# Combine stage of a two-layer pair-mixing kernel: the sum over k for all 256 rows at once, both halves of the product kept on chip

## What is computed

```python
zn = layer_norm(z)                                  # over c
a  = m * sigmoid(zn @ w_ag + b_ag) * (zn @ w_ap + b_ap)
b  = m * sigmoid(zn @ w_bg + b_bg) * (zn @ w_bp + b_bp)
p  = einsum('bikc,bjkc->bijc', a, b)                # for each c: a 256x256x256 product
x  = layer_norm(p) @ w_z + b_z
g  = sigmoid(zn @ w_g + b_g)
out = z + x * g                                     # residual added in this stage
```

## Time and profile before

| | |
|---|---|
| median of 3 executions (lowest, highest) | 2308.48 us (2306.16, 2319.19) |
| the profiled execution: its time, its span | 2298.41 us, 2296.6 us |
| combine of layer 0: first piece of b asked for, last `add` ends | 312.16, 646.19 us |
| the same for layer 1 | 1376.60, 1704.92 us |
| fill, 16 steps of layer 0 | 315.5 to 363.8 us |
| mixed, 48 steps of layer 0 | to about 582 us |
| drain, 16 steps of layer 0 | to 646.2 us |
| mean length of L919 (128x512 written with 64 floats between neighbours) | 1.066 us |
| mean length of L924 (128x512 written side by side) | 0.613 us |
| mean length of L242, whose neighbours in a pair lie 64 floats apart | 0.281 us |
| mean length of L493 (`conv_project`), whose neighbours in a pair lie 256 floats apart | 0.282 us |
| `fold_weights` of layer 0: its one DMA issued, first use, first matmul, last operation begins | 2.37, 4.91, 5.31, 6.79 us |

### The profile page before, as it was taken

The page is one execution under the profiler, slowest core; times in us unless marked ns, Lnnn a source line. Parts: engine busy times, 40 slices in busy tenths (PEclk is TensorE's granted clock), DMA queues, the critical chain, the costliest instruction groups (busy, mean ns, idle before and its releaser), DMA issues. The chain is left out here.

```text
span 2296.6 us, 44402 instructions
## 1 busy us (share of the span) xinstructions
PE 1752.8 (76%) x11740; PEld 1164.1 (51%) x11740; DVE 1584.8 (69%) x5005; ACT 1142.8 (50%) x2610; POOL 1168.2 (51%) x1594
## 2 busy tenths in 40 slices
PE   5778748888646659838887737978746999999998
PEld 3444437778522238724444426877734444444443
DVE  6888704566757768838787730665664889889887
ACT  5898813333125549817676633333216545555541
POOL 5777604676857740026566520766765343444330
PEclk9999979999779989959999979999885999999999
DMA  3777547888633314958789746988764555555552
GB/s 115 204 193 190 156 137 240 273 297 284 209 117 93 95 51 82 191 179 242 233 252 267 217 115 179 311 276 272 260 193 144 155 157 158 155 158 160 153 140 68
DMA packets 475473, 423.19 MB, mean 184 GB/s; under 512 B 224690, under 2 KB 372402, under 8 KB 475314
## 3 DMA queue, kind: packets, MB, share of 16 engines
q1 hardware_dynamic: 402610, 303.87, 47.4%
q10 hardware_dynamic: 72704, 117.47, 15.2%
HBM read 236.68 MB, written 150.99 MB: 169 GB/s over the span
## 5 line engine op out<-in xcount | busy, mean ns | idle before, releaser
L699 PE MATMUL cp_pv<-cp_weight,cp_zt 64*128 64x320 f32 x2048 | 369.8, 469 | 103.4 <-ACT cp_zt L637 87.8
L257 POOL TENSOR_TENSOR cc_ln_rstd<-cc_ln_var,numbers 128x8 f32<-128x8 f32 x128 | 255.5, 1996 | 188.5 <-DVE cc_ln_var L248 179.6
L523 DVE SCALAR_TENSOR_TENSOR a_res<-cp_pv,cp_mask,cp_sig 128x64 f32<-128x64 f32 x1024 | 263.9, 322 | 123.9 <-ACT cp_sig L646 119.4
L1537 DVE TENSOR_TENSOR ex_xe<-ex_spread,ex_xd 128x512 f32<-128x512 f32 x512 | 322.6, 683 | 36.0 <-PE ex_spread L1779 35.8
L829 PE MATMUL cc_sum<-a_res,cc_bch 128*128 (+1 forms) x2048 | 297.9, 296 | 62.6 <-DMA cc_bch<-b_scratch 59.3
L919 ACT ACTIVATE cc_p<-cc_sum 128x512 f32 (+1 forms) x128 | 135.8, 1061 | 376.4 <-PE cc_sum L829 239.7
L829 PEld LDWEIGHTS cc_sum<-a_res,cc_bch 128*128 128x128 f32 x2048 | 269.8, 205 | 85.0 <-issue 76.1
L646 ACT ACTIVATE cp_sig<-cp_pv 128x384 f32<-128x384 f32 x512 | 249.7, 493 | 125.7 <-PE cp_pv L699 124.0
L699 PEld LDWEIGHTS cp_pv<-cp_weight,cp_zt 64*128 64x128 f32 x2048 | 184.3, 189 | 222.3 <-issue 193.7
L1796 PE MATMUL ex_po<-ex_xe,ex_expert 128*64 128x512 f32 x1024 | 267.8, 647 | 0.1
L1589 POOL TENSOR_TENSOR ex_rstd<-ex_var,numbers 128x8 f32<-128x8 f32 x64 | 104.7, 1636 | 270.4 <-DVE ex_var L1485 260.5
(11 more groups left out here) (186 smaller groups left out, 2976.4 us busy)
## 6 DMA issues: line engine op xcount, KB each, us to landing
cc_bch<-b_scratch SPq DMA_DIRECT2D x256, 256.0 KB, 3.9
gate_scratch<-cp_sig SPq DMA_DIRECT2D x128, 256.0 KB, 2.6
b_scratch<-cp_b_stage SPq DMA_DIRECT2D x128, 256.0 KB, 4.0
cc_g<-gate_scratch ACTq DMA_DIRECT2D x128, 256.0 KB, 4.5
after_conv<-cc_p ACTq DMA_DIRECT2D x128, 256.0 KB, 3.8
ex_xd<-ex_xt SPq DMA_DIRECT2D x256, 128.0 KB, 2.5
cp_x<-in_x SPq DMA_DIRECT2D x64, 256.0 KB, 3.3
cc_p<-in_x ACTq DMA_DIRECT2D x64, 256.0 KB, 3.6
```

Of the source, the lines that this page charges most:

```text
L257: pool.tensor_tensor(rstd[q][:], var[q][:], numbers[:, 0:1].to_broadcast([P, tiles]), ALU.pow).then_inc(scaled if shifts else known, 1)
L523: dve.scalar_tensor_tensor(a_res[:, h, :, row], bank[:, h, 3 * C:4 * C], mask_sb[:, h, row:row + 1], sig[u.mod(2)][:, 0, h, i, :], ALU.mul ...
L699: pe.matmul(pv[slot(u, i)][:, h, 0:COLS], zt[u.mod(2)][half, i * P:(i + 1) * P], weight[half, :], start=True, stop=True).then_inc(v_made, 1)
L1537: dve.tensor_tensor(xe[u.mod(2)][:, :, h, i * P:(i + 1) * P], pb[2 * (p % 2) + h][:].rearrange("p (e t) -> p e t", e=EP), xd[u.mod(8)][:, ...
```

## The change

p is now cut into the two halves of j alone. For each half a piece of b (two channels, `CHUNKS` = 32 pieces) meets all 256 rows i: four matmuls with 256 columns, so each piece of b is read once instead of twice. The first half's p goes into `ptile` (now 256 rows), the second half's over half 0 of `a_res`, channel by channel as the products are done with it (`take_sums`), so with 256 floats between the channels of a row. There are three phases: 32 pieces alone; 32 steps with a piece of the second half beside the norm of eight rows of the first; 32 steps with the norm of the second half. Six buffers `room` of 128 x 512 serve b in the first phase; in the second two of them serve b, one `pn`, one `pt` and two g; in the third `pn` and `pt` have two each.

Per four steps (`QUAD`, 32 columns) DVE makes a first guess of 1/sqrt by integer operations (`first_guess`), and POOL refines it by three Newton rounds (`newton`, twelve small operations), in place of four powers. `measure` runs six steps ahead (`LEAD`). The fetch of x moves from ACT's queue to SP's. `prepare_weights` becomes `fold_projection`: one DMA of a packed array, one block. The loops are written out.

```diff
+def newton(pool, numbers, guess, half_var, root, rstd, done, base):
+    three_halves = numbers[:, 2:3].to_broadcast(list(rstd.shape))
+    for k in range(3):
+        was = guess if k == 0 else rstd
+        for j, (out, a, b, op) in enumerate([(root, was, was, ALU.mult), (root, root, half_var, ALU.mult),
+                                             (root, root, three_halves, ALU.subtract), (rstd, was, root, ALU.mult)]):
+            if j or k:
+                pool.wait_ge(done, base + 4 * k + j)
+            pool.tensor_tensor(out, a, b, op).then_inc(done, 1)
...
+        def p_rows(n, i, count):
+            at = n % STEPS * SR + i
+            if n < STEPS:
+                return ptile[:, at:at + count, :]
+            return a_res[:, 0, :, at:at + count].rearrange("p c i -> p i c")
...
+                for k in range(CHUNKS + 2):
+                    load_b(k)
+                for n in range(STEPS):
+                    load_x(n)
+                    if n + 2 < CHUNKS:
+                        load_b(CHUNKS + n + 2)
...
-                        for c in range(CH):
-                            at = (j * CH + c) * TI
-                            for k in range(H):
-                                ins = pe.matmul(psum[q][:, at:at + TI], bch[buf][:, k, :, c],
-                                                a_res[:, k, bass.ds(s * SC + j * CH + c, 1), ih * TI:(ih + 1) * TI],
-                                                start=k == 0, stop=k == H - 1)
...
+                    for c in range(CH):
+                        for half in range(H):
+                            ins = pe.matmul(psum[k % 3][:, c * N:(c + 1) * N], b[:, half, :, c],
+                                            a_res[:, half, k % CHUNKS * CH + c, :], start=half == 0, stop=half == H - 1)
...
+                for k in range(CHUNKS):
+                    add_up(k)
+                for n in range(STEPS):
+                    add_up(CHUNKS + n)
+                    if n:
+                        project(n - 1)
+                    flip(n)
+                project(STEPS - 1)
+                for n in range(STEPS, LAST):
+                    flip(n)
+                    if n > STEPS:
+                        project(n - 1)
+                project(LAST - 1)
...
+                for half in range(H):
+                    for n in range(half * STEPS, half * STEPS + LEAD):
+                        measure(n)
+                    for n in range(half * STEPS, (half + 1) * STEPS):
+                        scale(n)
+                        if n + LEAD < (half + 1) * STEPS:
+                            measure(n + LEAD)
+                        if n % STEPS:
+                            gate(n - 1)
+                    gate(n)
...
+                for half in range(H):
+                    refine(half * STEPS // 4)
+                    for n in range(half * STEPS, (half + 1) * STEPS):
+                        if n % 4 == 2 and n + 4 < (half + 1) * STEPS:
+                            refine(n // 4 + 1)
+                        if n % STEPS:
+                            add(n - 1)
+                    add(n)
...
+                for n in range(STEPS):
+                    take_sums(CHUNKS + n)
+                    take_flipped(n)
+                    if n:
+                        store(n - 1)
```

More of the change, by code:

```diff
@@ L135, in _ @@
                     ins.then_inc(centered, 1)
[L138 to L217, removed]
@@ L763, in chunk @@
-        def chunk(at, j):
-            turn, number = at
-            return (number + j) % BUFS, turn * (TURN * SUBS // BUFS) + (number + j) // BUFS
-        def now(part, r, t, q):
-            if r > 0:
-                half = t + (r - 1) * (STEPS // 2)
-                part(half * 2 + q, half, q, r - 1)
-        def behind(part, r, t, q, first):
-            if r > 0 and not (r == 1 and first):
-                half = t + (r - 1) * (STEPS // 2) - (1 - q)
-                part(half * 2 + 1 - q, half, 1 - q, r - 2 if first else r - 1)
@@ L780, in before @@
[L780 to L794 removed]
+        counted, guessed, refined = m.sem("counted"), m.sem("guessed"), m.sem("refined")
@@ L880, in body, with measure @@
-                def body(r, t, q, first, last, at):
-                    before(measure, r, t, q, last)
-                    now(scale, r, t, q)
-                    behind(gate, r, t, q, first)
-                rounds(dve, body)
-                at_end(gate)
+                def measure(n):
+                    dve.wait_ge(p_made, CHUNKS if n < STEPS else 2 * CHUNKS)
+                    if n % 4 == 0 and n:
+                        dve.wait_ge(guessed, n // 4 * 3 - 2)
+                    for i in range(0, SR, 2):
+                        ins = dve.bn_stats(stats[:, n % 4, i:i + 2, :].rearrange("p t s -> p (t s)"),
+                                           p_rows(n, i, 2).rearrange("p t c -> p c t"))
+                    ins.then_inc(counted, 1)
+                    if n % 4 == 3:
+                        first_guess(n // 4)
@@ L893, in add, with refine @@
[L893 to L904 removed]
+                def refine(quad):
+                    pool.wait_ge(guessed, quad * 3 + 3)
+                    if quad >= 2:
+                        pool.wait_ge(pn_made, (quad - 1) * 4)
+                    newton(pool, numbers, guess[:].bitcast(F32), half_var[:], root[:],
+                           rstd[quad % 2][:].rearrange("p n i -> p (n i)"), refined, quad * ROOTS)
@@ L936, in body @@
-                def body(r, t, q, first, last, at):
-                    if first:
-                        behind(store, r, t, q, first)
-                        if 2 <= r < len(TILES):
-                            act.wait_ge(stored, 16 * STEPS * (r - 1))
-                    if r < len(TILES):
-                        take_sums(r, t * 2 + q, q)
-                    now(take_flipped, r, t, q)
-                    if not first:
-                        behind(store, r, t, q, first)
-                rounds(act, body)
```

322 lines of the change are left out of this document (191 added, 131 removed).

## The result

The changed kernel took 2327.49 us (median, 2323.69 to 2337.52), the kernel before beside it 2307.32 (2304.51 to 2319.19): ratio 1.0084, 95% interval 1.0043 to 1.0126, slower by some 19 us. The prediction said 2318, range 2265 to 2350, slower the likeliest of the three.

The account below looks back on a forecast made before the run. The landing of g, in its buffer's two-step round, was taken to bound mixed steps. Layers of 342.1 us add 8.1 and 13.8, less 2 x 6.0: +9.9, 2308.3; with 10.1 from profiled execution to median, 2318, range 2265 to 2350.

Parts of the forecast that it names:

- First phase and the way to the second: Start of combine: 32 pieces alone at 1.73 us, 60.8 us, then 9.8 us from last product to first flip.
- Preparation: Weights made ready before combine: 8.0 us in place of 14.0, 6.0 less a layer.
- Second phase: 32 steps of products beside norm: POOL's Newton operations delay one `add` in four by 1.8 us; 3.8 a step, 119.8 us.
- Rival 4: Products beside norm: PE sets the step, 3.45 us for 3.8, 22 us less in all, 2296 us; chance 0.12.
- From the second to the third phase: Between norms of the two halves: 3.3 us to `gate`, then 8.5 for measure, guess, Newton and `scale`; 11.8 us.
- the tail: End of combine after the last norm steps: 5.0 us a layer.
- `scale` of the second half: DVE reading neighbours 256 floats apart: no extra cost taken; the other end was 0.46 us more a step.
- Rival 3: Norm of the second half: strided read costs `scale` 0.46 us in each of 64 steps, 29 us, 2347 us; chance 0.08.
- Third phase: 32 steps of norm alone on the second half: 4.35 us a step on average, 134.9 us a layer.
- two thirds of it at 4.69: Norm of the second half: two thirds at half clock, 4.69 us a step, one third at full clock, 3.66.
- Rival 2: Norm of the second half: half clock throughout, 4.69 us a step for 4.35, 10.5 a layer more, 2339 us; chance 0.20.
- Rival 1: Norm of the second half: PE stays at full clock, 3.66 us a step for 4.35, 21.4 a layer less, 2275 us; chance 0.22.

Follow-up runs that it names:

- the last versions: Changed kernel with all gainful edits and `scale` walking p four floats at a time, 0.9651; more g buffers, 0.9561; extra products too, 0.9575; all against the kernel before.
- the run with the clock held: Changed kernel with five extra 128-column PE products a step while the second half is normed; ratio 1.001 to the kernel before.
- the fastest version: Changed kernel with all gainful edits, four-float `scale` reads, and four g buffers from step 8 beside the second half's products; 2202.35 against 2302.33 us for the kernel before, 0.9561.

## Why the prediction was nearly right, and where it was not

The direction was right with the sum 7 to 9 us short in each layer; the table names the terms.

- **First phase and the way to the second:** 70.8 and 70.4 for 70.6. Pieces of 1.73 at a clock of 1.00 after the start, and 9.6 us from the last product of the first half to the first flip (forecast 9.8).
- **Preparation:** 6.0 a layer, shown by the run with nothing else changed.
- **Second phase:** 121.2 and 119.8 for 119.8, by the mechanism named. The block made the `add` 1.9 late, and both runs without the block took 4 to 9 us a layer off (the 4 alone would not be clear of the spread named above). Rival 4 (PE-bound, 3.45 a step) fell with it: a step took 3.9, 3.6 to 3.7 without the block, and 3.45 only with more buffers of g as well.
- **From the second to the third phase:** 15.4 and 17.3 for 11.8. The failed step is "Last flip, copy, projection, `gate`: 1.34 + 1.40 + 0.6 = 3.3". It let gate(31) wait for its projection only. It waited 5.11 us for g, with the measuring behind it on DVE. With the measuring ahead the term is 11.1 and 12.1. The same omission is in the tail (7.7 and 6.4 for 5.0), where the last `gate` waits 1.77 for g in layer 0 and 0.49 in layer 1; that was not tested by itself, and four buffers took 1 to 2 us off it.
- **`scale` of the second half:** the failed step is "I take nothing". It is 1.00 for 0.68, which is 9.9 us in 31 steps, and with neighbours read 11 us a layer went. Rival 3, given a chance of 0.08, had the right premise, at 0.32 instead of 0.46. The row it leaned on, L493, was a poor witness: it takes 0.28 us for 128 elements whatever it reads, 2.2 ns each, and so may hide a read that holds `scale` to 1.00 us for 512, 1.96 ns each; that it does is argued, no run tests it. The Trainium skill ("Advanced Engine Details and Errata", SBUF Cachelines) asks for two hits on a line of 16 bytes; the runs agree: single floats 1 KB apart 1.00 us, two floats of each 16 bytes 0.68 (`scale` in the last versions, four floats to a jump of 1 KB), whole neighbours 0.68. They don't tell floats to a line from floats to a jump.
- **Third phase:** 136.2 and 135.3 for 134.9 is luck, two errors that offset each other. The steps were priced right but for the stride (4.63 and 3.15 with neighbours read, forecast 4.69 and 3.18), and so was the block: the run with the clock held has three steps of 3.47 and a long one of some 5.5, 15.9 in four (over all its steps 16.2), and the forecast's 14.6 with 4 x 0.32 is 15.9. The failed step beside the stride is "two thirds of it at 4.69". By the granted clock some 17 and 16 steps of 31 ran at half clock and not 21, and that took off about as much as the stride put on. Rival 2, half clock throughout, fell with it: the clock came back several times in each layer, though PE waits in every step, and mostly fell again in a long step of 5.5 to 5.8. That is the course that the prediction described, and not that of the rule on oscillation as it put it for this rival.
- **Rival 1 priced full clock at 21.4 a layer.** Held at 0.97 the phase gave 10: 3.66 a step left out the stride (3.66 + 0.32 = 3.98, measured 4.05), while the phase that it starts from was short by the share of half clock.
- **What the prediction did not see:** it named POOL's block in two phases and took it as the price of the change. Newton's twelve operations are shorter than four powers, 3.9 against 6.6 us, and yet the powers win by 30 us a layer: 6 in the ways between the phases, where the first `scale` waits for one power instead of the whole block, and 24 in the second and third phases, 49 in both layers. Newton cut in three parts wins 42 there, though it is as many operations. It is the block that costs, not the operations.

## What to carry to other kernels

Price work by where it stands in its engine's queue, not by its length: the twelve operations in one block cost some 50 us in the two phases, and 12 more on the ways between them, that a longer but evenly spread power did not. At a change of phase, write down each operation that stands behind a wait it doesn't need; DVE stood still for 5 us ahead of a measuring that had all it needed. And before a row stands in for the cost of an access, ask whether its operation is fast enough to be held up by it.

## What was unexpected of the hardware

- What a strided DVE read costs depends on how much it takes at each place: two floats of each 16 bytes, four to a jump, are enough for 0.68 us, and one float to a jump costs 1.00.
- Turning p for this has a price on PE, which is in the measured time of the fastest version: there a weight load of the flip takes 0.21 us at full clock where it takes every fourth float, and 0.14 where it takes neighbours (its own second phase).
- The strided read is paid twice: the `add` on POOL that starts 0.16 us behind `scale` takes 1.65 behind a `scale` of 0.68 and 1.93 behind one of 1.00, alone 1.26. Min, median and max of the two phases of the changed kernel:

```profile
L854 POOL TENSOR_TENSOR cc_p<-cc_p,cc_room x30: 1267/1644/1711, 384.6 to 497.0; 128x512 f32<-128x512 f32 x30
L854 POOL TENSOR_TENSOR cc_p<-cc_p,cc_room x30: 1262/1923/1942, 519.7 to 649.3; 128x512 f32<-128x512 f32 x30
```

- The power of 8 columns took 1.64 us where the kernel before has a mean of 2.00 (groups by line and shape). It isn't whether DVE is quiet: in the kernel before, the 178 powers that begin while a `scale`, or the like operation of the next stage, runs on DVE take 2.01 to 2.13, and the 14 others 1.63 to 1.65. With one power a step all 128 took 1.63 to 1.65, with `gate`, measuring and even a whole `scale` beside them, but none began inside a `scale`.

```profile
L257 POOL TENSOR_TENSOR cc_ln_rstd<-cc_ln_var,numbers 128x8 f32<-128x8 f32 x128 | 255.5, 1996 | 188.5 <-DVE cc_ln_var L248 179.6
```

- A clock at 0.97 instead of 0.70 gave 10 us in 136; at 0.92 instead of 0.83, nothing that can be seen. What the clock costs depends on how much of a step's chain is PE's.
